# Two heads' maxima products side by side in TensorE's rows, stacks filled by 24 copies, y clipped by max(0, x)

## The chip, the cores and the metric

The kernel runs on one core of one Trainium2 chip. The metric is device time in microseconds of one execution of the whole program. TensorE (PE in the profile, PEld for its weight loads), VectorE (DVE), ScalarE (ACT) and GpSimd (POOL) compute; SyncE (SP) issues nearly all copies.

## The reference

For each of 32 batch entries (128 channels by 512 positions): layer norm over the positions, an attention of 8 heads of 16 channels against a context (rotary positions on half of each head's channels), a residual, a second layer norm, and a feed-forward block whose weights are rounded to -1, 0, 1 and whose activations are rounded to 8 bits.

```
q, k, v = project(layernorm(x)), project(ctx), project(ctx)    # 8 heads x 16 channels, T = 512
scores  = rope(q) . rope(k) / 4 ;  p = softmax(scores) ;  x += Wo (p v)
s       = 128 / max|x'|  per row ;  x'q = clip(round(x' s), -128, 127)     # x' = layernorm(x)
gate,up = x'q . ternary(Wg), x'q . ternary(Wu)       # 2048 columns
y       = fwht(silu(gate) * up)                      # Hadamard transform over 2048
out     = x + clip(round(y s), -128, 127) . ternary(Wd)
```

## The kernel before, in words

Each engine has one program, written out by hand as a list of calls in `step(t)`; a call names its batch entry (`t - 2`, `t + 1` and so on), and all engines walk through their steps in order. Four to five batch entries are in work at the same time. Nothing but semaphores ties the engines together, so the order within each list decides who waits for whom.

- **Products in bf16 pieces.** q and k are split into three bf16 parts each. Six copies of 16 rows (`Q_TERMS`, `K_TERMS`) stack them in `q_stack` and `k_stack`, so that one product over 96 rows gives the six largest cross terms. `stack_part` (L314) makes 12 copies of 128 KB per batch entry: six when part 0 is ready, four for part 1, two for part 2. Part 2 is the last one, made by GpSimd's `third_part` (L1321).
- **Maxima.** `score_max` (L439) multiplies the stacks for one head and 128 queries into a PSUM bank `s1[0]` or `s1[1]`, in turn; `reduce_scores` (L1009) on VectorE takes the row maximum. There are 32 of each per batch entry. `max_transpose` (L451) turns the maxima once all 32 are there, `max_out` (ScalarE) negates them, and `stack_max` (L334) copies them as row 97 of `q_stack`.
- **Softmax.** `scores` (L469) multiplies 97 rows, so that the maximum is already subtracted; ScalarE takes the exponential (L712); `weigh` (L484) multiplies by v. Each `weigh` is four products of 17 columns that run in four column strips of TensorE.
- **After the softmax.** `normalise` (L1019, L1022) on VectorE, `mix` (L1298) on GpSimd, `turn_back` (L1029) on VectorE, `attn_out` (L493) on TensorE, `residual` (L1040 to L1045) on VectorE, then quantisation of x, gate and up products (L525), `half_gates` (L1095), `glu` (L1104) on VectorE and `gate_product` (L1274) on GpSimd.
- **Hadamard transform.** GpSimd makes the outer four stages: `hadamard_half` (L1265, L1266) and `hadamard_last` (L1263); TensorE the inner seven (`hadamard`, L536). `y_out` (L764) brings them to SBUF, `quantise` (L1116 to L1120) finds the scale, `round_y` and `whole_y` (L753) round on ScalarE, `clip_y` (L1128) takes the minimum with 127 on VectorE, `y_transpose` (L547) and `down` (L560) follow.
- **Rotary positions.** `rope_sin` (L989), two copies that exchange 32-row blocks (`shift`, L326), `rope_cos` (L998), and GpSimd's `turn` (L1308), `rest` (L1315) and `third_part` (L1321) make the parts of the next batch entry.

GpSimd's list for one step is: `gate_product` 0 and 1, `hadamard_half` 0, `turn`, `gate_product` 2 and 3, `rest`, `hadamard_half` 1, `mix` 0, `third_part`, `mix` 1, `hadamard_last` 0 and 1, `rstd2`.

## Time and profile before

| what | value |
|---|---|
| median of 3 runs | 1534.24 us (1532.8 to 1534.24) |
| the profiled execution's own time | 1531.52 us |
| its span, first to last instruction | 1529.7 us |
| TensorE busy / VectorE / ScalarE / GpSimd | 1424.7 / 1322.4 / 1082.5 / 1098.7 us |
| mean granted TensorE clock | 0.974 of full |

The busy times are sums over the span; matmuls are pipelined, so two that follow each other overlap in their records, and a busy TensorE is not one at its peak. The span is a start of some 74 us up to the first transpose of maxima, 31 periods between such transposes, and an end of some 97 us.

### The profile page before, as it was taken

To read this page: it belongs to the slowest core of one execution; us is meant where nothing else is said; L and a number is where in the kernel's file an instruction comes from. 1 tells how busy PE (TensorE), PEld (TensorE's weight loads), DVE (VectorE), ACT (ScalarE), POOL (GpSimd) and SP (SyncE) were. 2 spreads that over 40 slices of the span, in tenths; PEclk is the share of its full clock that TensorE was granted. 3 is DMA by queue.
4 is the path that set the end of the run, shared out by engine and by line. 5 is a ranking of instruction groups with operands and counts; after the bars stand their busy time and mean duration, and the time that the engine had idled before them with its cause. 6 is when DMAs were issued, how large, how long until landed. Compare 5 with 4: busy or idle time off the path is not lost.

```text
span 1529.7 us, 30990 instructions
## 1 busy us (share of the span) xinstructions
PE 1424.7 (93%) x11042; PEld 743.8 (49%) x11042; DVE 1322.4 (86%) x2331; ACT 1082.5 (71%) x1777; POOL 1098.7 (72%) x812
## 2 busy tenths in 40 slices
PE   1688999999999999999999999999999999999983
PEld 1215455545555555455555544555555444555442
DVE  2768899999999999999999999999999999998641
ACT  3586677778777777787777777877777777777762
POOL 4124777887777778877777788777777887777674
PEclk9688999999999999999999999999999999999996
DMA  8861434434234344343244443332434443323000
GB/s 211 223 124 37 66 63 77 70 63 69 61 60 77 63 77 76 58 70 63 58 76 63 77 77 61 66 65 61 70 64 77 77 68 59 69 46 47 15 8 14
DMA packets 81112, 108.12 MB, mean 71 GB/s; under 512 B 9664, under 2 KB 59200, under 8 KB 79936
## 3 DMA queue, kind: packets, MB, share of 16 engines
q1 hardware_dynamic: 77744, 93.56, 35.4%
q10 hardware_dynamic: 3216, 12.58, 2.3%
q8 instruction: 89, 1.46, 0.4%
q14 instruction: 63, 0.52, 0.1%
HBM read 38.73 MB, written 8.39 MB: 31 GB/s over the span
## 4 chain that ended last, share of the span: by engine, by line
PE 71%; ACT 12%; DVE 5%; issue 4%; POOL 4%; DMA 2%; SPq 0%; POOLq 0%; ACTq 0%; DVEq 0%
PE s L469 12%; PE ring L525 12%; PE pv L484 12%; PE s L439 11%; PE ring L560 7%; PE ring L536 6%; ACT region L712 4%; PE ring L413 3%; PE ring L493 2%; ACT parts L779 2%; PE ring L547 2%; PE ring L427 2%; ACT y_last L753 1%; ACT y_last L771 1%; DVE maxima L1009 1%
## 5 line engine op out<-in xcount | busy, mean ns | idle before, releaser
L1009 DVE TENSOR_REDUCE maxima<-s 128x1 bf16<-128x512 f32 x1024 | 668.3, 682 | 60.1 <-PE s L439 55.6
L712 ACT ACTIVATE region<-s 128x512 f32<-128x512 f32 x1024 | 576.0, 597 | 133.3 <-PE s L469 123.8
L439 PE MATMUL s<-region 96*128 96x512 bf16 x1024 | 374.3, 391 | 21.7 <-DVE maxima L1009 11.5
L1274 POOL TENSOR_TENSOR region<-region,th 128x512 f32<-128x512 f32 x128 | 161.8, 1273 | 297.1 <-DVE th L1104 295.3
L469 PE MATMUL s<-region 97*128 97x512 bf16 x1024 | 362.2, 384 | 10.0 <-ACT region L712 4.8
L1265 POOL TENSOR_TENSOR region<-region 128x512 f32<-128x512 f32 x192 | 260.3, 1356 | 12.8
L484 PE MATMUL pv<-region,v_ext 128*17 128x512 f32 x2048 | 264.1, 599 | 0.0
L1266 POOL TENSOR_TENSOR region<-region 128x512 f32<-128x512 f32 x192 | 243.9, 1270 | 0.0
L439 PEld LDWEIGHTS s<-region 96*128 96x128 bf16 x1024 | 99.8, 98 | 198.6 <-DVE maxima L1009 74.2
L469 PEld LDWEIGHTS s<-region 97*128 97x128 bf16 x1024 | 93.2, 98 | 187.7 <-ACT region L712 154.1
L1263 POOL TENSOR_TENSOR region<-region 128x1024 f32<-128x1024 f32 x64 | 149.4, 2355 | 0.1
L794 ACT ACTIVATE v_ext<-ring 128x512 f32<-128x512 f32 x32 | 19.1, 598 | 180.7 <-PE ring L427 178.2
L536 PE MATMUL ring<-late_const,region 128*128 128x128 f32 x1024 | 132.7, 279 | 13.7 <-POOL region L1263 11.7
L525 PEld LDWEIGHTS ring<-xqT,wg 128*128 128x128 bf16 x2048 | 123.5, 98 | 42.5 <-issue 16.7
L525 PEld LDWEIGHTS ring<-xqT,wu 128*128 128x128 bf16 x2048 | 122.4, 98 | 44.7 <-issue 26.6
L525 PE MATMUL ring<-xqT,wg 128*128 128x128 bf16 x2048 | 136.0, 219 | 7.4 <-ACT xqT L721 6.9
L536 PEld LDWEIGHTS ring<-late_const,region 128*128 128x128 f32 x1024 | 129.0, 195 | 18.0 <-issue 13.6
L525 PE MATMUL ring<-xqT,wu 128*128 128x128 bf16 x2048 | 135.7, 219 | 2.2 <-ACT y_last L771 1.2
L560 PE MATMUL ring<-wd,y_last 128*128 128x512 bf16 x512 | 127.6, 382 | 1.6 <-ACT y_last L771 1.6
L1095 DVE TENSOR_TENSOR region<-ring,half_gate 128x512 f32<-128x512 f32 x128 | 87.5, 684 | 13.5 <-PE ring L525 9.5
L1308 POOL TENSOR_TENSOR region<-region,rope_c 64x1024 f32<-64x1024 f32 x32 | 75.6, 2362 | 31.5 <-DVE region L998 17.4
L1104 DVE SCALAR_TENSOR_TENSOR th<-th,ring 128x512 f32<-128x512 f32 x128 | 87.3, 682 | 5.5 <-PE ring L525 4.2
(104 smaller groups left out, 1812.0 us busy)
## 6 DMA issues: line engine op xcount, KB each, us to landing
region<-parts SPq DMA_DIRECT2D x384, 128.0 KB, 4.8
x_in<-in_x SPq DMA_DIRECT2D x32, 256.0 KB, 2.6
c_in<-in_ctx SPq DMA_DIRECT2D x32, 256.0 KB, 2.9
rope_c<-region SPq DMA_DIRECT2D x64, 128.0 KB, 2.4
x_res<-in_x SPq DMA_DIRECT2D x32, 256.0 KB, 2.6
out<-o_sb SPq DMA_DIRECT2D x32, 256.0 KB, 2.4
region<-in_wg_t ACTq DMA_DIRECT2D x1, 2048.0 KB, 9.2
region<-in_wu_t ACTq DMA_DIRECT2D x1, 2048.0 KB, 7.3
```

The source lines that it names most:

```text
L439: pe.matmul(s1[p][:, :], q_stack[k][0:STACK, h, 128 * c:128 * (c + 1)], k_stack[k][0:STACK, h, :], start=True, stop=True).then_inc(s1_full ...
L469: pe.matmul(s2[n % 2][:, :], k_stack[k][0:STACK + 1, h, 128 * c:128 * (c + 1)], q_stack[k][0:STACK + 1, h, :], start=True, stop=True).then ...
L484: last = pe.matmul(pv[32 * i:32 * i + DH + 1, :], v_ext[b % 2][:, c, 4 * g + i, :], probs[:, (4 * u + i) % 8, :], start=(c == 0), stop=(c ...
L525: last = pe.matmul(bank(f"{name}{j}")[:, 128 * i:128 * (i + 1)], w[:, c, o:o + 128], xqT[:, c, :], start=(c == 0), stop=(c == HC - 1), ski ...
L536: last = pe.matmul(bank(f"y{j}")[:, 128 * c:128 * (c + 1)], z[:, o:o + 128], had[:, :], start=True, stop=True, skip_group_check=True)
L560: last = pe.matmul(bank("down")[:, :], yqT[:, c, :], wd[:, c, :], start=(c == 0), stop=(c == IC - 1))
L712: act.activation(probs[:, n % 8, :], s2[n % 2][:, :], ACT.Exp, scale=SCALE).then_inc(exp_done, 1)
L1009: dve.reduce_max(maxima[:, c, h:h + 1], s1[p][:, :], AXX).then_inc(s1_max[p], 1)
L1263: return pool.tensor_tensor(o[:, :, half, :], a[:, :, 0, :], a[:, :, 1, :], ALU.subtract if half else ALU.add)
L1265: pool.tensor_tensor(o[:, :, 0, :], a[:, :, 0, :], a[:, :, 1, :], ALU.add)
L1266: return pool.tensor_tensor(o[:, :, 1, :], a[:, :, 0, :], a[:, :, 1, :], ALU.subtract)
L1274: pool.tensor_tensor(zj, zj, th[:, j % 2, :], ALU.mult).then_inc(glu_done, 1)
```

## The change

Seven things change together.

- The maxima use only the four largest cross terms, which fill 64 rows. Heads 0 to 3 have theirs in rows 0 to 63 of the stacks, heads 4 to 7 in rows 64 to 127, and `score_max` issues two products, one in each half of TensorE's rows, into the two PSUM banks. It waits for both banks first.
- The other two terms of heads 0 to 3 lie in rows 64 to 95, and those of heads 4 to 7 in rows 32 to 63. The maximum is row 96 for the former and row 31 for the latter; rows 0 to 31 of the latter's `q_stack` are set to zero once. `scores` multiplies 97 or 128 rows.
- Each copy of `stack_part` becomes two of half the size (24 in all), `shift` issues four copies and covers all 128 rows, `stack_max` issues two. `rope_sin` and `turn` work on 128 rows.
- `whole_y` and `clip_y` become one ScalarE instruction, `below_top`, which writes max(0, top - y) with top = ROUND + 127; `yT_out` turns that back with scale -1 and bias 127.
- For the last batch entry, VectorE does the second half of the gate products and of the Hadamard stages (`tail_half`).
- GpSimd fills the first two stacks completely at the start, not one row of them.
- The lists of all engines are in a new order, and the PSUM ring is assigned anew.

```diff
-STACK_DMAS = 2 * len(Q_TERMS)
-SHIFTS = 2
+STACK_DMAS = 4 * len(Q_TERMS)
+SHIFTS = 4
+MAX_ROW = (STACK, 31)
+ROWS = (slice(0, STACK + 1), slice(0, 128))
+MAIN = (slice(0, 4 * DH), slice(4 * DH, 8 * DH))
+HALF = NH // 2
+def term_rows(g, r):
+    lo = DH * r if g == 0 else 64 + DH * r if r < 4 else 32 + DH * (r - 4)
+    return slice(lo, lo + DH)
+def heads(g):
+    return slice(HALF * g, HALF * (g + 1))
...
                         if terms[r] == part:
-                            sp.dma_start(dst[DH * r:DH * (r + 1), :, :], parts[:, part, w, :]).then_inc(stacked, 16)
+                            for g in range(2):
+                                sp.dma_start(dst[term_rows(g, r), heads(g), :],
+                                             parts[64 * g:64 * (g + 1), part, w, :]).then_inc(stacked, 16)
...
-                wait(pe, s1_max[p], 16 * b + i)
-                pe.matmul(s1[p][:, :], q_stack[k][0:STACK, h, 128 * c:128 * (c + 1)],
-                          k_stack[k][0:STACK, h, :], start=True, stop=True).then_inc(s1_full[p], 1)
+                for g in range(2):
+                    wait(pe, s1_max[g], 16 * b + i)
+                for g in range(2):
+                    h = HALF * g + i // KC
+                    pe.matmul(s1[g][:, :], q_stack[k][MAIN[g], h, 128 * c:128 * (c + 1)],
+                              k_stack[k][MAIN[g], h, :], start=True, stop=True).then_inc(s1_full[g], 1)
...
-                pe.matmul(s2[n % 2][:, :], k_stack[k][0:STACK + 1, h, 128 * c:128 * (c + 1)],
-                          q_stack[k][0:STACK + 1, h, :], start=True, stop=True).then_inc(s2_full, 1)
+                rows = ROWS[h // HALF]
+                pe.matmul(s2[n % 2][:, :], k_stack[k][rows, h, 128 * c:128 * (c + 1)], q_stack[k][rows, h, :],
+                          start=True, stop=True).then_inc(s2_full, 1)
...
-            def whole_y(b, j):
+            def below_top(b, j):
...
-                act.activation(yq[:, 1024 * j:1024 * (j + 1)], ys[:, 1024 * j:1024 * (j + 1)], ACT.Copy, bias=-ROUND) \
-                   .then_inc(whole, 1)
+                act.activation(yq[:, 1024 * j:1024 * (j + 1)], ys[:, 1024 * j:1024 * (j + 1)], ACT.Relu, scale=-1.0,
+                               bias=top[:, :]).then_inc(yq_done, 1)
...
+            def tail_half(b):
+                if b != B - 1:
+                    return
+                for j in (2, 3):
+                    moved(dve, f"gate{j}", b)
+                    moved(dve, f"up{j}", b)
+                    zj = z[:, 512 * j:512 * (j + 1)]
+                    dve.tensor_tensor(zj, zj, th[:, j % 2, :], ALU.mult).then_inc(tail_steps, 1)
+                dve.wait_ge(tail_steps, 2)
+                dve.wait_ge(had16_done, 2 * b)
+                for stage in range(3):
+                    butterfly(dve, stage, 1).then_inc(tail_steps, 1)
+                    dve.wait_ge(tail_steps, 3 + stage)
+                dve.wait_ge(had8_steps, 6 * b + 3)
+                butterfly(dve, 3, 1).then_inc(tail_done, 1)
...
-                pool.memset(k_stack[k][STACK:STACK + 1, :, :], 1.0).then_inc(ones_rows_set, 1)
...
+                    pool.memset(k_stack[k][:, :, :], 1.0).then_inc(ones_rows_set, 1)
+                    pool.memset(q_stack[k][0:32, heads(1), :], 0.0).then_inc(ones_rows_set, 1)
```

The first place is VectorE's list from the transpose of the mixed attention (`turn_back`) to the statistics of the residual. Before, it reads as follows; `maxima<-s_0` and `maxima<-s_1` are `reduce_scores` from the two banks, `o_sb` is the store of the entry before.

```order
1041 L1009 TENSOR_REDUCE maxima<-s_1 128x1
1042 L1009 TENSOR_REDUCE maxima<-s_0 128x1
1043 L1029 STREAM_TRANSPOSE attn<-mixed 128x512
1044 L1136 SCALAR_TENSOR_TENSOR o_sb<-ring,sc,h_res 128x512
1045 L1009 TENSOR_REDUCE maxima<-s_1 128x1
1046 L1040 SCALAR_TENSOR_TENSOR h_res<-ring,out_bias,x_res 128x512
1047 L1042 BN_STATS st<-h_res 128x6
1048 L1043 BN_AGGR mv<-st 128x2
1049 L1045 TENSOR_SCALAR ve<-mv 128x1
1050 L1009 TENSOR_REDUCE maxima<-s_0 128x1
1051 L1051 TENSOR_REDUCE sc<-turned_pv 128x1
```

In the changed kernel the same stretch of VectorE's list reads:

```order
1019 L1037 TENSOR_REDUCE maxima<-s_0 128x1
1020 L1037 TENSOR_REDUCE maxima<-s_1 128x1
1021 L1057 STREAM_TRANSPOSE attn<-mixed 128x512
1022 L1174 SCALAR_TENSOR_TENSOR o_sb<-ring,sc,h_res 128x512
1023 L1037 TENSOR_REDUCE maxima<-s_0 128x1
1024 L1037 TENSOR_REDUCE maxima<-s_1 128x1
1025 L1068 SCALAR_TENSOR_TENSOR h_res<-ring,out_bias,x_res 128x512
1026 L1070 BN_STATS st<-h_res 128x6
1027 L1071 BN_AGGR mv<-st 128x2
1028 L1073 TENSOR_SCALAR ve<-mv 128x1
1029 L1037 TENSOR_REDUCE maxima<-s_0 128x1
1030 L1079 TENSOR_REDUCE sc<-turned_pv 128x1
```

Between `turn_back` and `residual` there stood one reduction, and now there stand two. From there up to the first `glu` both lists hold the same instructions in a slightly other order, with four reductions in each.

The second place is TensorE's list around the transpose of the maxima (`eye_b,maxima`). Before:

```order
1048 L439 MATMUL s_1<-region 128x512
1049 L493 MATMUL ring<-attn,late_const 128x512
1050 L427 MATMUL ring<-table_const,c_in 128x128 x4
1051 L536 MATMUL ring<-late_const,region 128x128 x4
1052 L451 MATMUL ring<-eye_b,maxima 8x128 x4
1053 L439 MATMUL s_0<-region 128x512
1054 L536 MATMUL ring<-late_const,region 128x128 x4
1055 L439 MATMUL s_1<-region 128x512
1056 L439 MATMUL s_0<-region 128x512
1057 L536 MATMUL ring<-late_const,region 128x128 x8
```

In the changed kernel, with the waits of each instruction in brackets (a matmul that waits stands in a row apart from those behind it in its group):

```order
1120 L480 MATMUL s_0<-region 128x512 [waits s1_max1,s1_max0]
1121 L480 MATMUL s_1<-region 128x512
1122 L531 MATMUL ring<-attn,late_const 128x512 [waits attn_done,ring_free1]
1123 L577 MATMUL ring<-late_const,region 128x128 [waits had16_done,ring_free2]
1124 L577 MATMUL ring<-late_const,region 128x128 x3
1125 L492 MATMUL ring<-eye_b,maxima 8x128 [waits s1_max1,s1_max0,ring_free0]
1126 L492 MATMUL ring<-eye_b,maxima 8x128 x3
1127 L480 MATMUL s_0<-region 128x512 [waits s1_max1,s1_max0,stacked]
1128 L480 MATMUL s_1<-region 128x512
1129 L577 MATMUL ring<-late_const,region 128x128 [waits had16_done,ring_free1]
```

The maxima products now come in pairs behind one wait for both banks. The first pair of a batch entry stands ahead of the second Hadamard group, as its single product did, and waits for all copies of that entry's stacks.

The third place is SP's list for one batch entry, before:

```order
104 L334 DMA region<-neg_max 1x8x512
105 L297 DMA x_res<-in_x 128x512
106 L326 DMA rope_c<-region 32x1024 x2
107 L341 DMA out<-o_sb 128x512
108 L314 DMA region<-parts 16x8x512 x12
```

and in the changed kernel:

```order
100 L362 DMA rope_c<-region 32x1024 x4
101 L349 DMA region<-parts 16x4x512 x24
102 L371 DMA region<-neg_max 1x4x512 x2
103 L331 DMA x_res<-in_x 128x512
104 L379 DMA out<-o_sb 128x512
```

SP issues 30 copies for shifts, stacks and maxima of one entry, where it issued 15.

## Rows read from the trace of the kernel before

**Rows 1.** The page: busy us (share of the span) and instructions of two engines

```profile
PE 1424.7 (93%) x11042; PEld 743.8 (49%) x11042; DVE 1322.4 (86%) x2331; ACT 1082.5 (71%) x1777; POOL 1098.7 (72%) x812
```

**Rows 2.** One period: busy us (instructions) per engine, clock, DMA; then all maxima transposes

```profile
951.50:995.10 43.60, 43.07 (x345) 22.59 (x343) 40.60 (x73) 32.35 (x54) 33.99 (x27) 1.00 0.38 68
L451 PE MATMUL ring<-eye_b,maxima x128: 219/219/314, 73.9 to 1432.9; 128*8 128x128 bf16 x128
```

**Rows 3.** Timeline of TensorE around one `weigh` and two products of maxima and scores

```profile
702.92 0.38 PE L469 MATMUL s<-region 97*128 97x512 bf16 x1
703.23 1.05 PE L484 MATMUL pv<-region,v_ext 128*17 128x512 f32 x8
704.21 1.07 PE L525 MATMUL ring<-xqT,wu 128*128 128x128 bf16 x16
...
705.12 0.38 PE L439 MATMUL s<-region 96*128 96x512 bf16 x1
705.34 0.38 PE L469 MATMUL s<-region 97*128 97x512 bf16 x1
```

**Rows 4.** Timeline of VectorE from `turn_back` to the first `glu`

```profile
951.64 0.71 DVE L1029 STREAM_TRANSPOSE attn<-mixed 128x512 f32<-128x512 f32 x1
...
956.12 0.69 DVE L1009 TENSOR_REDUCE maxima<-s 128x1 bf16<-128x512 f32 x1 [0.43 <-PE s L439]
...
964.17 0.68 DVE L1009 TENSOR_REDUCE maxima<-s 128x1 bf16<-128x512 f32 x1
964.77 0.68 DVE L1095 TENSOR_TENSOR region<-ring,half_gate 128x512 f32<-128x512 f32 x1
965.37 0.68 DVE L1104 SCALAR_TENSOR_TENSOR th<-th,ring 128x512 f32<-128x512 f32 x1
```

**Rows 5.** Timeline of GpSimd from the first gate product to behind the second `mix`

```profile
966.19 2.60 POOL L1274 TENSOR_TENSOR region<-region,th 128x512 f32<-128x512 f32 x2 [9.01 <-DVE th L1104]
...
974.02 1.80 POOL L1265 TENSOR_TENSOR region<-region 128x512 f32<-128x512 f32 x1
975.79 1.26 POOL L1266 TENSOR_TENSOR region<-region 128x512 f32<-128x512 f32 x1
...
995.07 4.67 POOL L1263 TENSOR_TENSOR region<-region 128x1024 f32<-128x1024 f32 x2
```

**Rows 6.** Groups over 19 periods: busy us, mean ns, idle before

```profile
L1308 POOL TENSOR_TENSOR region<-region,rope_c 64x1024 f32<-64x1024 f32 x19 | 44.9, 2363 | 1.5
...
L1128 DVE TENSOR_SCALAR y_last<-y_last 128x1024 bf16<-128x1024 bf16 x38 | 44.6, 1175 | 0.0
```

**Rows 7.** SP's copies of part 2 in one period, and TensorE's first maxima product

```profile
L314 SPq DMA_DIRECT2D region<-parts x2: 546/573/600, 951.0 to 951.6; - x2
...
DMA to landing us min/median/max: 3.3/3.4/3.5
955.62 0.39 PE L439 MATMUL s<-region 96*128 96x512 bf16 x1
```

**Rows 8.** Start: fills and first rstd on GpSimd, the first stack's copies, their landing

```profile
1.27 7.07 POOL L1233 MEMSET region<- 1x4096 bf16 x2
...
24.24 7.77 SPq L314 DMA_DIRECT2D region<-parts  x12
DMA to landing us min/median/max: 3.4/5.9/8.5
L1240 POOL MEMSET region<- x1: 3516/3516/3516, 94.5 to 94.5; 128x4096 bf16 x1
```

**Rows 9.** End: the last Hadamard half on VectorE's and GpSimd's timeline, then TensorE

```profile
1488.40 0.69 DVE L1104 SCALAR_TENSOR_TENSOR th<-th,ring 128x512 f32<-128x512 f32 x1 [1.31 <-PE ring L525]
...
1492.28 2.49 POOL L1274 TENSOR_TENSOR region<-region,th 128x512 f32<-128x512 f32 x2
...
1502.53 4.64 POOL L1263 TENSOR_TENSOR region<-region 128x1024 f32<-128x1024 f32 x2
1505.01 6.42 PE L536 MATMUL ring<-late_const,region 128*128 128x128 f32 x32 [11.32 <-POOL region L1263]
```

496 lines of the change are left out of this document (241 added, 255 removed).

## The prediction

> **What bounds the kernel now.** I read the page's busy table first, then one steady period by windows, then the timelines of three engines over that period, and last the start and the end.
>
> The page puts TensorE first (93%) and VectorE close behind [rows 1]. In a steady period of 43.6 us they are busy 43.07 and 40.60 us [rows 2], so both are nearly full, while ScalarE and GpSimd have 10 us to spare. The first transpose of maxima stands 73.9 us into the span, the last at 1432.9 [rows 2]: 31 periods with a mean of 43.8, a little over the steady 43.6.
>
> A full engine is not yet the bound. GpSimd idles once per period, 9.01 us, for the first `glu` [rows 5], and from there it works without a break until the second `mix` ends. That closes a loop. `turn_back` on VectorE starts at 951.64, the first `glu` at 965.37 [rows 4], the first gate product at 966.19, and `hadamard_last`, which follows the second `mix`, at 995.07 [rows 5]. The next `turn_back` needs that `mix`. From 951.64 to 966.19 is 14.55 us, from 966.19 to 995.07 is 28.88, and some 0.15 us of handing over make 43.58: the whole period. The only idle time shown inside it is 0.43 us on VectorE, where the first reduction waits for TensorE [rows 4]. So the kernel has two bounds of the same size, TensorE's list and this loop, and the reader should see that relieving one alone brings nothing.
>
> **TensorE, the pairs.** Two products of 512 columns stand 0.22 us apart [rows 3], so a pair of them costs 0.44 us, and 16 pairs 7.0 us per period. Side by side they cost 0.22 and save 3.5 us per period, if changing to half rows is free. The nearest row to what such a change costs is `weigh`, the step into four column strips: it starts 0.31 us behind the product ahead, not 0.22 (0.09 more), and what follows starts 0.98 us later, though eight f32 products in two rounds of four are worth 0.86 by the spacing of two 0.43 us rounds (0.12 more) [rows 3]. The 0.43 is my estimate for an f32 product of 512 columns, twice the bf16 spacing. By that row a pair costs 0.22 + 0.09 + 0.12 = 0.43 us, what it costs today. Six of the 16 pairs stand next to a `weigh` or the transpose, where one change serves both, 0.1 us each. So the pairs save between 0.6 us (change charged) and 3.5 us (free) per period. I take 0.6, since the row for columns is the nearest.
>
> The Trainium skill, TensorEngine Tiling (Array Packing), Key Properties, says that going from one tiling mode to another drains the array; the 0.09 and 0.12 us agree for column strips, and no row here shows it for row halves. By that rule the saving is the 0.6; by the same page's ideal of twice the speed it would be the 3.5.
>
> **VectorE.** Two clips go. They cost 44.6 us over 19 periods, 2.35 per period [rows 6], and VectorE falls to about 38.3. One of them also lies inside the loop: one `hadamard_half` instruction takes 1.80 us where its neighbour takes 1.26 [rows 5], because a clip of 0.4 us starts in it. That is -0.53 in the loop. `turn` takes 2.36 us on 64 rows [rows 6], and `hadamard_last` with as many columns on 128 rows 4.67 for two [rows 5], so `turn`, and by the same reason `rope_sin`, costs nothing more on 128 rows; `below_top` has the size of `whole_y`.
>
> **The loop.** One more reduction stands between `turn_back` and `residual`: +0.60 us, the spacing of two such instructions [rows 4]. The idle 0.43 us depends on the first maxima product, at 955.62 [rows 7]. It now waits for four copies of part 2, not two. They are issued about 0.6 us apart, the second at 951.6, and land up to 3.5 us later [rows 7]; the fourth lands at 951.6 + 1.2 + 3.5 = 956.3, 0.7 us later than the product started. Since VectorE also comes 0.6 us later, the idle time stays near 0.5. If the half-size copies land sooner the idle time vanishes. So the loop is 43.58 + 0.60 - 0.53, then +0.1 or -0.4: 43.2 to 43.8. I take 43.5, near the upper half, since 24 issues and two more for the maxima keep SP busier. TensorE's list needs about 43.0 by the charged price, and is covered by the loop. The steady part gives 31 x (43.5 - 43.56) = -2 us (bounds -11 to +7).
>
> Pairs also end the alternation of banks: VectorE idles from the end of one pair to the arrival of the next, about 0.5 us, where no other work stands between. The list has four such places, 2 us, and none is inside the loop; VectorE has 5 us to spare, so I cost it at nothing. If that cover went, it would be those 2 us a period.
>
> **The start.** GpSimd fills two single rows in 7.07 us before the first rstd [rows 8]. A fill of all 128 rows takes the same 3.5 us each [rows 8], but two fills of 2048 columns come on top, by halves 1.8 us each: +3.6. The first stack's 12 copies are issued over 7.77 us and the last lands 8.5 us after its issue [rows 8], so 39.9; 24 copies take 15.5 us to issue and the last then lands about 3.4 us later, 43.1, plus what started late, 47; but the weights' traffic, which slowed the old ones, is over by then. Between +2 and +7; I take +4.
>
> **The end.** VectorE takes the second half of the last entry. The last `glu` starts at 1488.40, GpSimd begins the second half at 1492.28 and ends the third stage at 1502.53, TensorE starts at 1505.01 [rows 9]. VectorE needs 8 instructions of 0.60 and one of about 1.2, so 6.0 us, from 1489.1 to about 1495.5; GpSimd's first half has ended by 1492.28 [rows 9]. Then one last stage each, 2.3 us on GpSimd: TensorE starts near 1497, 8 us sooner. The bound against it: the 1.80 us instruction shows that the two engines can block each other [rows 5]; if they take turns throughout, TensorE starts near 1501, 4 us sooner. A gain of 3 us more is possible if TensorE's clock holds: its 32 products take 6.42 us here. I take -8 (bounds -4 to -11).
>
> The Trainium skill, SBUF — State Buffer, SBUF: two separate sides, says that VectorE with two SBUF inputs and GpSimd exclude each other for whole instructions. By it the end would give the 4 us. The trace shows such a stop for the clip alone.
>
> **The sum.** 1531.5 + 4 - 2 - 8 = 1525.5 for the profiled execution. The median of the runs lies 2.7 us above that execution, so 1528. What this kernel's measurement can tell from no change is about 0.2%, 3 us.
>
> **The rivals.**
>
> - *The relief of TensorE counts in full.* The pairs are free and the loop is softer than I read it. TensorE's list falls to 43.56 - 3.5 = 40.1, VectorE to 38.3. If the period gets half way, 41.8, the time is 1528 - 31 x 1.7 = 1475. For it: TensorE is 99% busy; against it: the loop adds up to the period without rest.
> - *The change of mode costs more for rows than for columns.* The second half's weights of 128 columns are loaded behind the change. TensorE's list decides once it passes the loop's 43.5, that is when a pair costs over 0.46. At 0.50 the list is 44.1: 1528 + 31 x 0.6 = 1547. For it: `weigh` loads only 17 columns per strip and still pays; against it: six neighbours share a change.
> - *Copies come late.* If a copy of half size lands no faster than a whole one, 24 of them at 1.1 us, the spacing I estimate from the growing delays of the first stack (3.4 to 8.5 us over 12 copies issued 0.65 apart), take 26 us of the period, the first product waits some 4 us, and 31 x 3 makes 1620.
> - *The pairs don't overlap at all.* Then each costs 0.65, the list 46.9, and the time 1528 + 31 x 3.4 = 1633.
>
> **Chances.** Loop-bound as forecast 0.48, with a range of its own of 1517 to 1540; full relief 0.20; dearer change of mode 0.22; late copies 0.06; no overlap 0.04. The range that leaves out 2 in 10 goes from 1480 to 1555. Faster: 0.31 of the forecast's share, all of the relief and a little, 0.53; same 0.14; slower 0.33.
>
> **What would show it.** Right: the period stays between 43.2 and 43.8 while VectorE's busy time per period drops by 2 us; GpSimd still waits about 9 us for the first `glu` and for nothing else; the pair's two products start within 0.02 us of each other, 0.31 us behind the one ahead; the instruction of 1.80 us is 1.27; TensorE's last Hadamard group starts 8 us nearer to its gate products. Wrong: a period under 43, or GpSimd idle at another place; TensorE without gaps and a period over 44; waits for the copies at the first pair.

## The result, and the profile of the changed kernel

The changed kernel took 1540.81 us (median of 5 runs, 1538.71 to 1543.81), the kernel before 1532.8 us (5 runs, 1531.79 to 1534.24). The ratio is 1.0051, 95% interval 1.0034 to 1.0068: slower, by half a per cent. The profiled execution took 1540.81 us, over a span of 1539.0 us.

The page's table of busy times, which answers to [rows 1], and the lines that make up the chain that ended last:

```profile
PE 1383.7 (90%) x11042; PEld 698.3 (45%) x11042; DVE 1264.9 (82%) x2277; ACT 1100.2 (71%) x1777; POOL 1077.0 (70%) x806
...
SPq L349 16%; PE ring L563 13%; PE s L507 9%; PE pv L522 7%; PE s L480 6%; PE ring L451 4%; DVE maxima L1037 3%; DMA region<-parts 3%; POOL region L312 2%; POOL region L311 2%; PE ring L577 2%; DMA rope_c<-region 2%; PE ring L601 1%; ACT re
```

TensorE has 41 us less to do and VectorE 57.5 us less, and the kernel is slower. L349, SyncE's 24 copies, makes up 16% of the chain. One period by windows, and all transposes of maxima (L492 is what L451 was), as in [rows 2]:

```profile
702.00:745.50 43.50, 42.12 (x346) 21.31 (x345) 38.58 (x71) 32.99 (x54) 33.38 (x26) 1.00 0.24 73
L492 PE MATMUL ring<-eye_b,maxima x128: 218/219/314, 85.7 to 1447.1; 128*8 128x128 bf16 x128
```

TensorE and VectorE are each a microsecond or two freer within a period of the same length. With the starts of the transposes the span falls into four pieces:

| piece | before | changed | difference | predicted |
|---|---|---|---|---|
| up to the first transpose | 73.9 | 85.7 | +11.8 | |
| first three periods together | 140.1 | 138.3 | -1.8 | start as a whole +4 |
| the other 28 periods | 1218.7 | 1222.9 | +4.2 | -2 |
| from the last transpose on | 97.0 | 92.1 | -4.9 | -8 |

The sum is +9.3 us, the difference of the spans (1529.7 and 1539.0). Of the +4.2 us, 1.6 lie in 24 periods of 43.66 us (43.59 before) and 2.6 in the last four, two of which take 44.22 and 44.97 us; no run looks into those. The prediction's error of 15.3 us (1525.5 for the profiled execution, 1540.8 measured) is 6 at the start, 6 in the periods and 3 at the end.

**The period.** VectorE from `turn_back` (L1057) to the first `glu` (L1132), which answers to [rows 4]:

```profile
701.49 0.70 DVE L1057 STREAM_TRANSPOSE attn<-mixed 128x512 f32<-128x512 f32 x1
...
702.77 1.29 DVE L1037 TENSOR_REDUCE maxima<-s 128x1 bf16<-128x512 f32 x2
...
705.84 0.69 DVE L1037 TENSOR_REDUCE maxima<-s 128x1 bf16<-128x512 f32 x1
...
709.05 0.54 DVE L1008 TENSOR_SCALAR xn<-x_in,mv,rs 128x512 f32<-128x512 f32 x1
709.51 0.42 DVE L1109 TENSOR_SCALAR xq<-turned_pv 128x512 bf16<-128x512 f32 x1
...
715.24 0.68 DVE L1132 SCALAR_TENSOR_TENSOR th<-th,ring 128x512 f32<-128x512 f32 x1
```

and GpSimd, as in [rows 5]; the first line is the second `mix` of the kernel before, which followed GpSimd's work without a wait, and the others are the changed kernel's:

```profile
994.49 0.61 POOL L1298 TENSOR_TENSOR mixed<-turned_pv,inv_sum 128x256 f32<-128x256 f32 x1
...
700.52 0.62 POOL L1327 TENSOR_TENSOR mixed<-turned_pv,inv_sum 128x256 f32<-128x256 f32 x1 [0.40 <-DVE inv_sum L1050]
...
716.07 2.51 POOL L1299 TENSOR_TENSOR region<-region,th 128x512 f32<-128x512 f32 x2 [9.01 <-DVE th L1132]
...
723.81 1.27 POOL L311 TENSOR_TENSOR region<-region 128x512 f32<-128x512 f32 x1
```

From `turn_back` to the gate product it is 14.58 us, as it was (14.55); the means between 300 and 1250 us are 14.68 and 14.56. The third of GpSimd's stages, which took 1.80 us beside a clip, takes 1.27 (723.81). The wait of 0.43 us ahead of the first reduction is gone (705.84 follows without a gap), a reduction came in, and `xn`, the normalised x of the next entry, stands ahead of `xq`, where it stood behind `quantise` before. On GpSimd the second `mix` now waits 0.40 us (0.24 us a period by the waits view from 400 to 1200) for `inv_sum`, which VectorE makes once TensorE's last `weigh` of the entry is done.

That wait shows a second loop, which the prediction did not follow: from `turn_back` over `xq` and TensorE's list to the last `weigh`, and over `inv_sum` and the second `mix` back to the next `turn_back`. Its legs, from start to start, are means over the entries whose `turn_back` lies between 350 and 1200 us:

| leg, mean us | before | changed | g3_xq_first | h1_combined |
|---|---|---|---|---|
| `turn_back` to `xq` (VectorE) | 7.51 | 8.10 | 7.75 | 7.63 |
| `xq` to its transposes (TensorE) | 0.56 | 0.57 | 0.57 | 0.57 |
| transposes to the last `weigh` | 32.32 | 32.25 | 32.30 | 32.30 |
| last `weigh` to `inv_sum` | 1.41 | 1.41 | 1.41 | 1.41 |
| `inv_sum` to the second `mix` | 1.04 | 0.38 | 0.41 | 0.46 |
| second `mix` to the next `turn_back` | 0.73 | 0.95 | 0.92 | 0.91 |

Before, `inv_sum` was ready some 0.7 us before GpSimd came to it (1.04 less the 0.38 that the handing over takes where GpSimd waits). The reduction and `xn` ahead of `xq` have taken that up, and GpSimd now waits.

TensorE around the first pairs of an entry (L480 the pairs, L492 the transpose of maxima, L539 that of xq), beside [rows 3, 7]:

```profile
704.66 0.39 PE L492 MATMUL ring<-eye_b,maxima 128*8 128x128 bf16 x4
705.20 0.39 PE L480 MATMUL s<-region 64*128 64x512 bf16 x2 [0.16 <-DMA region<-parts]
705.52 2.94 PE L577 MATMUL ring<-late_const,region 128*128 128x128 f32 x24
708.84 0.60 PE L507 MATMUL s<-region 97*128 97x512 bf16 x2 [0.37 <-DMA region<-neg_max]
710.07 0.38 PE L539 MATMUL ring<-eye_b,xq 128*128 128x128 bf16 x4 [0.63 <-DVE xq L1109]
...
710.67 0.39 PE L480 MATMUL s<-region 64*128 64x512 bf16 x2
710.99 0.61 PE L507 MATMUL s<-region 97*128 97x512 bf16 x2
```

A pair is two products in one row of 0.39 us, which start 2 to 6 ns apart, and the next instruction starts 0.32 us after it. What TensorE now waits for in 800 us (400 to 1200), by the waits view: line, what it waited for, us in total, times, longest:

```profile
PE ring L539 <- DVE xq L1109: 16.3, 19, 1.3
PE s L480 <- DMA region<-parts: 5.7, 11, 1.1
...
PE s L507 <- DMA region<-neg_max: 2.6, 8, 0.8
```

The kernel before has two rows there, 3.5 us for `xqT` and 0.2 us for the maxima. The relief of TensorE, about 1 us a period, is spent in waits: 0.9 us for `xq`, 0.3 us for copies of the stacks.

**The start**, beside [rows 8]; L362 are the shifts, L1337 the rotation, L349 the copies:

```profile
7.15 0.42 ACTq L290 DMA_DIRECT2D region<-in_wg_t  x1
...
17.67 2.92 SPq L362 DMA_DIRECT2D rope_c<-region  x4
...
25.20 2.34 POOL L1337 TENSOR_TENSOR region<-region,rope_c 128x1024 f32<-128x1024 f32 x1 [12.88 <-DMA rope_c<-region]
28.76 15.27 SPq L349 DMA_DIRECT2D region<-parts  x24
...
51.20 0.39 ACTq L290 DMA_DIRECT2D region<-in_wd_t  x1
...
56.17 2.46 SPq L362 DMA_DIRECT2D rope_c<-region  x4
...
67.33 2.34 POOL L1337 TENSOR_TENSOR region<-region,rope_c 128x1024 f32<-128x1024 f32 x1 [24.44 <-DMA rope_c<-region]
...
76.12 1.87 PE L418 MATMUL pv<-absum,ones 128*128 128x1 f32 x8 [3.28 <-ACT wu L716]
```

The first stack is 5.9 us later (its first product at 45.88, before at 39.97): the rotation starts 4.5 us later (25.20, before 20.75), and the 24 copies add the rest. From there to the first transpose another 5.9 us are lost. The second entry's rotation starts at 67.33; in the kernel before it started at 54.57, ahead of the down weights:

```profile
50.27 1.21 SPq L326 DMA_DIRECT2D rope_c<-region  x2
54.57 2.33 POOL L1308 TENSOR_TENSOR region<-region,rope_c 64x1024 f32<-64x1024 f32 x1 [17.43 <-DVE region L998]
60.47 0.39 ACTq L269 DMA_DIRECT2D region<-in_wd_t  x1
```

**The end**, beside [rows 9]; L1142 are VectorE's gate products, L309 the last stage:

```profile
1497.05 2.50 POOL L1299 TENSOR_TENSOR region<-region,th 128x512 f32<-128x512 f32 x2 [8.81 <-DVE th L1132]
...
1504.56 2.36 DVE L1142 TENSOR_TENSOR region<-region,th 128x512 f32<-128x512 f32 x2
1504.78 1.59 POOL L311 TENSOR_TENSOR region<-region 128x512 f32<-128x512 f32 x1
1506.33 1.71 POOL L312 TENSOR_TENSOR region<-region 128x512 f32<-128x512 f32 x1
1506.95 1.64 DVE L311 TENSOR_TENSOR region<-region 128x512 f32<-128x512 f32 x1
...
1512.02 3.29 POOL L309 TENSOR_TENSOR region<-region 128x1024 f32<-128x1024 f32 x1 [3.98 <-DVE region L312]
1515.46 5.81 PE L577 MATMUL ring<-late_const,region 128*128 128x128 f32 x32 [5.26 <-POOL region L309]
```

### The profile page after: what moved, and what is told of

Its sections match the earlier page's. It is cut to its first block, busy times and chain, and to the rows that moved or that the text cites. A ratio compares the mean times of both kernels' runs of the same rounds, so it can differ in the third digit from the quotient of the medians.

```text
span 1539.0 us, 31895 instructions
## 1 busy us (share of the span) xinstructions
PE 1383.7 (90%) x11042; PEld 698.3 (45%) x11042; DVE 1264.9 (82%) x2277; ACT 1100.2 (71%) x1777; POOL 1077.0 (70%) x806
## 4 chain that ended last, share of the span: by engine, by line
PE 45%; SPq 17%; DVE 10%; POOL 9%; issue 7%; ACT 6%; DMA 5%; POOLq 0%; DVEq 0%; ACTq 0%
SPq L349 16%; PE ring L563 13%; PE s L507 9%; PE pv L522 7%; PE s L480 6%; PE ring L451 4%; DVE maxima L1037 3%; DMA region<-parts 3%; POOL region L312 2%; POOL region L311 2%; PE ring L577 2%; DMA rope_c<-region 2%; PE ring L601 1%; ACT region L737 1%; ACT parts L806 1%
## 5 line engine op out<-in xcount | busy, mean ns | idle before, releaser
L1037 DVE TENSOR_REDUCE maxima<-s 128x1 bf16<-128x512 f32 x1024 | 660.8, 683 | 122.4 <-PE s L480 114.8
L507 PE MATMUL s<-region 128*128 128x512 bf16 (+1 forms) x1024 | 356.2, 387 | 22.1 <-DMA region<-neg_max 12.9
L311 POOL TENSOR_TENSOR region<-region 128x512 f32<-128x512 f32 x189 | 240.4, 1272 | 12.5
L480 PE MATMUL s<-region 64*128 64x512 bf16 x1024 | 204.1, 394 | 42.0 <-DVE maxima L1037 24.0
L312 POOL TENSOR_TENSOR region<-region 128x512 f32<-128x512 f32 x189 | 241.2, 1276 | 0.0
L507 PEld LDWEIGHTS s<-region 128*128 128x128 bf16 (+1 forms) x1024 | 89.8, 97 | 251.5 <-ACT region L737 147.7
L480 PEld LDWEIGHTS s<-region 64*128 64x128 bf16 x1024 | 50.8, 93 | 226.6 <-issue 140.4
L309 POOL TENSOR_TENSOR region<-region 128x1024 f32<-128x1024 f32 x63 | 147.9, 2368 | 4.0 <-DVE region L312 4.0
L791 ACT ACTIVATE region<-ring 128x512 f32<-128x512 f32 x128 | 75.7, 592 | 95.6 <-PE ring L577 95.2
L577 PEld LDWEIGHTS ring<-late_const,region 128*128 128x128 f32 x1024 | 121.1, 194 | 35.2 <-issue 27.8
L1337 POOL TENSOR_TENSOR region<-region,rope_c 128x1024 f32<-128x1024 f32 x32 | 75.4, 2357 | 48.9 <-DMA rope_c<-region 47.0
L761 ACT ACTIVATE th<-region 128x512 f32<-128x512 f32 x128 | 80.4, 628 | 27.0 <-DVE region L1123 26.9
```

The lines of the kernel that those rows point to most:

```text
L309: return engine.tensor_tensor(o[:, :, half, :], a[:, :, 0, :], a[:, :, 1, :], ALU.subtract if half else ALU.add)
L311: engine.tensor_tensor(o[:, :, 0, :], a[:, :, 0, :], a[:, :, 1, :], ALU.add)
L312: return engine.tensor_tensor(o[:, :, 1, :], a[:, :, 0, :], a[:, :, 1, :], ALU.subtract)
L480: pe.matmul(s1[g][:, :], q_stack[k][MAIN[g], h, 128 * c:128 * (c + 1)], k_stack[k][MAIN[g], h, :], start=True, stop=True).then_inc(s1_full ...
L507: pe.matmul(s2[n % 2][:, :], k_stack[k][rows, h, 128 * c:128 * (c + 1)], q_stack[k][rows, h, :], start=True, stop=True).then_inc(s2_full, 1)
L577: last = pe.matmul(bank(f"y{j}")[:, 128 * c:128 * (c + 1)], z[:, o:o + 128], had[:, :], start=True, stop=True, skip_group_check=True)
```

## The experiments

Each is an edit of the changed kernel (one, and its extension, of the kernel before). The time of the kernel before, run beside them, had medians of 1533.1 to 1534.2 us. "First" is the start of the first transpose of maxima in the profiled execution, "period" the mean of the 24 periods from the fourth on, both from the starts of those transposes. One profiled execution gives the period to about 0.05 us: edits that touch the start alone left it between 43.64 and 43.74. The start scatters more: f1, g3 and h2, whose edits don't touch what the first transpose needs, have it at 84.5, 84.8 and 86.7, so a difference of 1 us in that column says nothing.

| kernel | median us | ratio to before, 95% | first | period |
|---|---|---|---|---|
| before | 1532.8 | 1 | 73.9 | 43.59 |
| changed | 1540.8 | 1.0034 to 1.0068 | 85.7 | 43.66 |
| e1_split_first | 1541.4 | 1.0035 to 1.0063 | 85.2 | 43.74 |
| e2_split_all | 1539.6 | 1.0028 to 1.0055 | 84.6 | 43.68 |
| e3_late_fills | 1537.5 | 1.0013 to 1.0034 | 84.7 | 43.64 |
| e4_full_rows | 1550.9 | 1.0104 to 1.0132 | 86.0 | 44.02 |
| f1_fewer_products | 1534.3 | 0.9994 to 1.0011 | 84.5 | 43.58 |
| f2_reductions_later | 1594.9 | 1.0364 to 1.0402 | 86.6 | 45.38 |
| f3_four_more_issues | 1666.5 | 1.0838 to 1.0873 | 89.0 | 47.84 |
| f4_four_from_scalar | 1662.2 | 1.0817 to 1.0846 | 86.1 | 47.75 |
| g1_late_load_split | 1536.1 | 1.0011 to 1.0029 | 79.8 | 43.72 |
| g2_two_from_scalar | 1536.3 | 1.0012 to 1.0031 | 82.2 | 43.59 |
| g3_xq_first | 1531.0 | 0.9972 to 0.9990 | 84.8 | 43.37 |
| g4_clip_alone | 1529.8 | 0.9974 to 0.9993 | 74.6 | 43.49 |
| h1_combined | 1522.5 | 0.9906 to 0.9934 | 80.8 | 43.26 |
| h2_no_tail | 1544.1 | 1.0056 to 1.0084 | 86.7 | 43.68 |
| h3_before_clip_tail | 1524.1 | 0.9927 to 0.9952 | 73.9 | 43.49 |
| h4_combined_fewer | 1517.3 | 0.9874 to 0.9904 | 79.9 | 43.12 |

**e1_split_first.** The first suspicion for the start was the wait for both banks: with no other work on VectorE a pair came only every 2.06 us (VectorE's reductions at 46.52 and 48.58).

```diff
-                for g in range(2):
-                    wait(pe, s1_max[g], 16 * b + i)
+                if b > 0:
+                    for g in range(2):
+                        wait(pe, s1_max[g], 16 * b + i)
                 for g in range(2):
+                    if b == 0:
+                        wait(pe, s1_max[g], 16 * b + i)
```

> The changed kernel; for the first entry alone each product for the maxima waits only for its own bank, right before it, not for both banks ahead of both. Theory (the start lost the alternation of banks: pairs 2.06 us apart where 1.36 would do): the first transpose of maxima comes 4 to 6 us sooner than 85.7 and the time falls by as much, 1535 to 1537, periods unchanged. Rival (at the start the low clock and the row mode of the products set the pace, not the wait for both banks): under 1 us, 1540 to 1541.

The reductions then came every 1.39 us per pair, and nothing was gained: after the last of them VectorE waited 8.3 us for the next pair, which stands in TensorE's list behind the sum over the up weights.

```profile
59.65 9.04 DVE L1040 TENSOR_REDUCE maxima<-s 128x1 bf16<-128x512 f32 x13
...
75.61 1.87 PE L418 MATMUL pv<-absum,ones 128*128 128x1 f32 x8 [7.65 <-ACT wu L719]
...
78.06 1.29 DVE L1040 TENSOR_REDUCE maxima<-s 128x1 bf16<-128x512 f32 x2 [8.29 <-PE s L483]
```

The theory falls: the wait for both banks is real, but another wait covers it.

**e2_split_all.** The same for all entries.

```diff
-                for g in range(2):
-                    wait(pe, s1_max[g], 16 * b + i)
                 for g in range(2):
+                    wait(pe, s1_max[g], 16 * b + i)
```

> The changed kernel with the wait of each bank right before its own product, for all entries, so that two products need not start together. Theory (the steady periods are set by the chain of copies, loop and GpSimd, and VectorE's wait for pairs has slack): the start gains as in the first experiment and the period stays within 0.05 us of 43.66: 1534 to 1537. Rival (the lost alternation costs 0.1 us a period and more): period 43.5 or less, 1530 or less. Second rival (two products that no longer overlap cost TensorE 0.1 to 0.2 us for each of 16 neighbours and TensorE's list is the bound): period 44.5 or more, 1560 or more.

1539.6 us and a period of 43.68: neither the alternation nor the common start matters at this size. The 1 us of the median is within what the runs scatter.

**e3_late_fills.** GpSimd fills behind its first power of the variance.

```diff
-                ones_rows(t + 6, 0)
-                ones_rows(t + 6, 1)
                 rstd1(t + 1)
+                ones_rows(t + 1, 0)
+                ones_rows(t, 1)
```

> The changed kernel; GpSimd fills the rows of ones of the first two stacks behind its first power of the variance, not ahead of it. Theory (the fills delay the first entry by 3.3 us): first transpose of maxima 2.5 to 3.5 us sooner, 1537 to 1538.5. Rival (the first stack is set by the 24 issues and what is ahead of them, and the fills now come between GpSimd's power and its sum): no gain, 1540 to 1542.

The power came at 5.37, not 11.77, and the rotation at 25.00, not 25.20:

```profile
5.37 0.56 POOL L1282 TENSOR_TENSOR rs<-ve,half_neg 128x1 f32<-128x1 f32 x1 [4.23 <-DVE ve L1001]
...
5.97 5.44 DVE L1008 TENSOR_SCALAR xn<-x_in,mv,rs 128x512 f32<-128x512 f32 x1 [0.77 <-POOL rs L1282]
...
16.18 2.58 SPq L362 DMA_DIRECT2D rope_c<-region  x4
25.00 2.34 POOL L1337 TENSOR_TENSOR region<-region,rope_c 128x1024 f32<-128x1024 f32 x1 [13.88 <-DMA rope_c<-region]
```

GpSimd fills from 5.88 to 11.12. VectorE's L1008, 0.55 us elsewhere, took 5.44 us: it ended about when the two fills did. And the shifts were issued 1.5 us sooner and still landed at 25.0, while 4 MB of gate weights (issued from 7.58 on) came in. So 1.5 of the 3.3 us by which the shifts are issued later than before (17.67, before 14.34) cost the first stack next to nothing: sooner issues met the same traffic. No run leaves the fills out altogether, and what the other 1.8 us cost isn't shown. The median is 3.3 us lower; the first transpose is 1.1 us sooner, which is within its scatter, and where the rest comes from isn't shown.

**e4_full_rows.** The maxima from all six terms, over 96 or 128 rows.

```diff
+FULL = (slice(0, STACK), slice(0, 128))
-                    pe.matmul(s1[g][:, :], q_stack[k][MAIN[g], h, 128 * c:128 * (c + 1)],
-                              k_stack[k][MAIN[g], h, :], start=True, stop=True)
+                    pe.matmul(s1[g][:, :], q_stack[k][FULL[g], h, 128 * c:128 * (c + 1)],
+                              k_stack[k][FULL[g], h, :], start=True, stop=True)
```

> The changed kernel, but each product for the maxima reads 96 rows (heads 0 to 7) or all 128 (heads 8 to 15), six terms rather than the four largest, so that two products cannot lie side by side and no row mode is entered or left; the rows ahead of heads 8 to 15 add an old maximum, so the maxima of these heads differ from the reference's. Theory (the loop and not TensorE's list bounds the period): 16 pairs cost 0.44 rather than 0.41, TensorE's busy time rises by 0.3 to 0.6 us a period and the period by 0.3 at most: 1541 to 1552. Rival (TensorE's list bounds it): the period rises by the whole, and if lying side by side is worth what two 0.22 us products in the time of one are worth (3.5 us a period), to 47: 1640.

Period +0.36 us, 10 us in all. By windows from 400 to 1200 TensorE is busy 775.46 us (42.67 a period) here and 770.85 us (42.07) in the changed kernel. Lying side by side is thus worth 0.6 us of TensorE's time a period, as the prediction took it, and not 3.5. TensorE's leg of the second loop is 32.66 us, 0.41 longer, and the second `mix` waits 9.1 us in 800, not 4.4.

**f1_fewer_products.** 0.9 us less for TensorE; a quarter of the down projection's sum is left out.

```diff
-                down(t - 4, 4, 8)
```

> The changed kernel without four of the 16 products of the down projection, so that its sums lack a quarter: 0.9 us less on TensorE's list in a period, nothing else. If TensorE's list is the bound: period 42.8, 1513. If a loop that runs through other engines is (VectorE and GpSimd, or the 24 copies): the four products stood in a stretch that waits anyway, period within 0.2 of 43.6, 1535 to 1541.

Period 43.58, 0.08 below. Of the 6.5 us by the medians, 2.3 lie behind the last transpose (89.8 us, not 92.1); another 1.2 lie ahead of the first, where none of these products stands, and are scatter. About half of what went came back as a new wait, 8.6 us in 800 for exponentials, and TensorE's leg of the second loop is only 0.13 us shorter (32.12). So the sum of TensorE's work doesn't set the period of the changed kernel; what counts is the time from `xq` to the last `weigh`.

**f2_reductions_later.** Two reductions out of the loop.

```diff
                 half_gates(t - 2, 0)
-                reduce_scores(t, 2)
                 round_piece(t - 2, 2, 6)
-                reduce_scores(t, 3)
                 half_gates(t - 2, 1)
                 glu(t - 2, 0)
                 round_piece(t, 0, 3)
+                reduce_scores(t, 2)
+                reduce_scores(t, 3)
```

> The changed kernel; VectorE's reductions 2 and 3 come behind its first product of tanh and up, not ahead of it, which takes 1.2 us out of the loop from the turned back attention to GpSimd's first gate product. If that loop bounds the period: 43.1 to 43.3, 1526 to 1531. If the 24 copies or TensorE's list bound it: no change of the period, 1539 to 1542, or 0.1 to 0.5 us worse where TensorE's next pair waits for the reductions that come later, up to 1557.

54 us slower, more than either side expected. The waits of TensorE from 400 to 1200:

```profile
PE s L480 <- DVE maxima L1037: 32.8, 36, 1.7
```

TensorE's waits for reductions are 1.9 us a period, where they were 0.2, and the period grew by 1.7. That doesn't test the loop; it shows that with one wait for two banks, a reduction can't be put off past the next pair.

**f3_four_more_issues.** The same bytes in 28 copies.

```diff
-STACK_DMAS = 4 * len(Q_TERMS)
+STACK_DMAS = 4 * len(Q_TERMS) + 4
...
+                                if part == 0 and r < 2 and w == 0:
+                                    lo = term_rows(g, r).start
+                                    for j in range(2):
+                                        sp.dma_start(dst[lo + 8 * j:lo + 8 * (j + 1), heads(g), :],
+                                                     parts[64 * g + 32 * j:64 * g + 32 * (j + 1), part, w, :]) \
+                                          .then_inc(stacked, 16)
+                                    continue
```

> The changed kernel; four of part 0's copies are cut into halves, so that SyncE issues 28 copies of the same bytes rather than 24: at 0.63 us an issue the last lands 2.5 us later. If the chain of copies bounds the period (the first pair waits 0.16 us for the last copy): period +2.4, 1615. If the loop through VectorE and GpSimd does and the first pair can be late without harm: under +0.3 a period, up to 1550. In between if the pair's lateness eats other slack first.

Each period is 4.2 us longer: more than the 2.5 us of the issues. TensorE's waits from 400 to 1200, then its timeline:

```profile
PE s L487 <- DMA region<-parts: 56.2, 17, 4.1
...
763.91 0.39 PE L487 MATMUL s<-region 64*128 64x512 bf16 x2 [2.77 <-DMA region<-parts]
764.23 4.57 PE L584 MATMUL ring<-late_const,region 128*128 128x128 f32 x24
```

The first pair waits 3.4 us a period for copies, and behind such a wait the 24 Hadamard products take 4.57 us, where the changed kernel took 2.94. The granted clock, 1.00 in that stretch of the changed kernel, is 0.63 from 763.90 to 768.50 here and 1.00 on either side: behind this idle time of 2.8 us TensorE runs for a while at the lower of its two levels, 1.2 rather than 2.4 GHz. The 2.5 us of the issues and the 1.6 us of the slower products nearly make up the 4.2. So the copies had no slack (0.16 us of waiting in the period shown), and here a late copy costs its lateness and two thirds again.

**f4_four_from_scalar.** Four copies issued by ScalarE.

```diff
+                                if part == 0 and r < 2 and w == 0:
+                                    continue
...
+            def act_copies(b):
...
+                for r in range(2):
+                    for g in range(2):
+                        act.dma_start(q_stack[slot(b)][term_rows(g, r), heads(g), :],
+                                      parts[64 * g:64 * (g + 1), 0, 0, :]).then_inc(stacked, 16)
...
                 first_part(t + 1)
+                act_copies(t + 1)
```

> The changed kernel; four of part 0's copies are issued by ScalarE right behind its first part, not by SyncE, so that the last copy lands 2.5 us sooner and ScalarE's queue is 1.6 to 2.5 us fuller at its weak spot. If the chain of copies bounds the period: 43.2 to 43.4, 1527 to 1534. If it doesn't: period unchanged, 1535 to 1541 (the first stack may still be 2 us sooner at the start), or worse where the exponentials behind the issues are awaited.

The waits for copies are gone (0.2 us in 800), and 44.7 us for exponentials came in their place. ScalarE's timeline has the reason:

```profile
742.39 2.50 ACTq L822 DMA_DIRECT2D region<-parts  x4
744.94 2.98 ACT L739 ACTIVATE region<-s 128x512 f32<-128x512 f32 x5 [2.68 <-issue]
```

Four issues hold ScalarE's whole list for 2.7 us at a place where TensorE's next scores wait for exponentials. The second `mix` then waits 58.1 us in 800 for `inv_sum`, and the period is 4.1 us longer: the rival, at its dearest.

**g1_late_load_split.** With e1's edit, the first 2 MB of the down weights are loaded later.

```diff
-                load_weights(t, 2, 0)
                 round_y(t - 3, 1)
...
                 first_part(t + 1)
+                load_weights(t, 2, 0)
```

> The changed kernel with the split waits of the first entry, and the first half of the down weights (2 MB) loaded behind the second entry's first part in ScalarE's order, not ahead of it. Theory (the first transpose of maxima is late since the second entry's shifts, 56.2 to 58.6, share the DMA engines with that load of 51.2 and land at 67.3; ScalarE then stands at the first part, and the sum over the up weights behind it): shifts land before 63, first transpose of maxima at 79 to 82 in place of 85.7, 1534 to 1538. Rival (the up weights alone fill the DMA engines, the shifts land no sooner): 85, 1539 to 1541.

```profile
54.16 2.74 SPq L362 DMA_DIRECT2D rope_c<-region  x4
...
61.39 2.34 POOL L1340 TENSOR_TENSOR region<-region,rope_c 128x1024 f32<-128x1024 f32 x1 [20.03 <-DMA rope_c<-region]
```

From the first issue to the rotation it is now 7.2 us, not 11.2; the issue itself is 2.0 us sooner. With e1's edit alone the issue was 0.8 us sooner (55.37) and the rotation stood at 66.8. The first transpose stands at 79.8, 5.9 us sooner, as much as had been lost between the first stack and it. The time fell by 4.7.

**g2_two_from_scalar.** Two copies of part 2 in ScalarE's idle time ahead of `v_out`, with the same waits as in f4 and one for part 2.

```diff
+                            if part == 2 and w == 1:
+                                continue
...
+                act_copies(t)
                 v_out(t)
```

> The changed kernel; two of the four copies of part 2 are issued by ScalarE in its idle time of 3.4 us ahead of the values' copy, the other two by SyncE, so that the last lands 1.2 us sooner and nothing waits behind ScalarE's two. Theory A (two chains are equal within 0.2 us in a period: copies, and VectorE with GpSimd; 28 issues made each period 4.1 us longer, so the copies have no slack): the waits of pairs for copies (0.3 us a period) go, period 43.3 to 43.6, 1528 to 1539. Theory B (the copies alone bound the period): 42.6 or less, 1510. Rival (issuing from ScalarE costs what its exponentials lose, as with four of part 0): over 1545.

4.5 us faster than the changed kernel, 3.5 of them before the first transpose (82.2) and at most 0.07 us a period. 0.07 us is hardly above the scatter of the period. Theory A stands as far as this goes; the same kind of edit as f4, at another place of the same list, costs nothing that shows.

**g3_xq_first.** One line moved.

```diff
                 gate_factors(t - 2)
-                norm1_apply(t + 1)
                 quant_x(t - 2)
+                norm1_apply(t + 1)
```

> The changed kernel; VectorE rounds the attention's sum to xq ahead of the next entry's normalised x, not behind it: the loop from the turned back attention through xq, its transposes and gate 0 to GpSimd's first gate product is 0.46 us shorter, nothing else moves. If that loop bounds the period alone: 43.2, 1527. If the copies are as tight (theory of two equal chains): 43.4 to 43.66, 1532 to 1541.

9.8 us faster than the changed kernel, period 43.37, so 0.29 of the 0.46 us came through. It did not come where the expectation had it: from `turn_back` to the first gate product the mean is 14.75 us (14.68 in the changed kernel), for VectorE still does the same work there. What became shorter is `turn_back` to `xq`, 7.75 rather than 8.10 us; TensorE's wait for `xq` over 800 us fell from 16.3 to 10.5 us, and the second `mix` no longer waits for `inv_sum`. This is the clearest test of the second loop: an edit that moves 0.46 us within VectorE's list, at 38.6 busy of 43.5, is worth more than 0.9 us off TensorE.

**g4_clip_alone.** In the kernel before.

```diff
-                act.activation(yq[:, 1024 * j:1024 * (j + 1)], ys[:, 1024 * j:1024 * (j + 1)], ACT.Copy, bias=-ROUND) \
-                   .then_inc(whole, 1)
+                act.activation(yq[:, 1024 * j:1024 * (j + 1)], ys[:, 1024 * j:1024 * (j + 1)], ACT.Relu, scale=-1.0,
+                               bias=top[:, :]).then_inc(yq_done, 1)
...
-                clip_y(t - 3, 1)
...
-                clip_y(t - 2, 0)
```

> The kernel before with one part of the change: y is clipped by ScalarE's max(0, x) and VectorE's two minima of a period go (2.35 us of VectorE), all else in its old order. Theory (VectorE has slack and the minima stand outside the loop but for what they excluded GpSimd, 0.5 us): period 43.1 to 43.56, 1517 to 1534. Rival (no slack anywhere, VectorE's whole time counts): 41.2 bounded by TensorE's 43.07, 1517 or less.

3.3 us faster than the kernel before that ran beside it (1529.8 and 1533.1), period 43.49. VectorE loses 2 us of work a period, and 0.1 comes through. GpSimd is done sooner: from the first gate product to the end of the second `mix` it takes 0.5 us less, but `turn_back` then starts 0.57 us behind that end, not 0.11. It follows reductions in VectorE's list, and these wait for TensorE (60.9 us in 800, before 21.6), which is busy 42.9 of 43.49 us. That TensorE's list holds the rest back is read from these waits; no run tests it.

**h1_combined.** The edits of e1, e3, g1, g2 and g3 together.

> The changed kernel with the five edits that each gave something or were free: xq ahead of the normalised x, two copies from ScalarE, the late load of down weights, split waits for the first entry, the late fills. If they add: start 79 to 80 or less in place of 85.7, period 43.2 to 43.3, 1522 to 1526. If one resource is left right behind them (TensorE's list of about 43.1, or the copies), the period stays at 43.3 and more and only the start adds: 1525 to 1530.

1522.5 us: 18 us below the changed kernel and 0.8% below the kernel before. TensorE's waits from 400 to 1200:

```profile
PE ring L544 <- DVE xq L1129: 9.7, 18, 0.8
PE s L512 <- DMA region<-neg_max: 4.4, 18, 0.3
```

No pair waits for copies any more. The start adds less than hoped (80.8), the periods add in full (43.26). The second `mix` waits for nothing here: `turn_back` to the first gate product takes 14.65 us, from there to the next `turn_back` 28.62, and the sum of 43.27 is the predicted loop again.

**h2_no_tail.** The last entry's second half back on GpSimd.

```diff
-                tail_half(t - 2)
...
-                if b == B - 1 and j > 1:
-                    pe.wait_ge(tail_done, 1)
-                else:
-                    pe.wait_ge(had16_done, 2 * b + 1 + j // 2)
+                pe.wait_ge(had16_done, 2 * b + 1 + j // 2)
```

> The changed kernel with GpSimd alone for the last entry's second half, as before the change. Theory (the shared tail saved 4.8 us between the gate products and the last Hadamard products): end 4 to 5 us longer, 1544 to 1546. Rival (the shorter end comes from elsewhere): 1540 to 1542.

The stretch behind the last transpose is 97.1 us, as before the change (97.0) and not 92.1. The shorter end is the tail's, all of it. By the medians the kernel is 3.3 us slower than the changed one, somewhat less than the 5.0 us of this stretch.

**h3_before_clip_tail.** g4's kernel with `tail_half` as in the changed one.

> The kernel before with the clip by ScalarE's max(0, x) and the last entry's second half on VectorE, but 96 rows for each head, one head at a time, 12 copies and the old orders. Theory (these two parts gain 3.3 and 4 to 5 us, and the pairs with their copies and orders lose what is left of the change): 1524 to 1527. Rival (the two gains overlap or the tail's needs the new order): 1528 to 1531.

1524.1 us. Two small parts of the change, without the pairs, the 24 copies and the new orders, make the kernel 0.6% faster; what the rest adds to them is 17 us.

**h4_combined_fewer.** The combined kernel with f1's edit.

> The combined kernel without four of the 16 products of the down projection (its sums lack a quarter): 0.9 us less on TensorE's list in a period. If after the shorter loop TensorE's list of 43.1 is what stands next: period 42.5 to 42.8, some 15 us below the combined one. If copies or the loop do: period within 0.2 of the combined one, 0 to 6 us below it.

5.2 us below the combined one, period 43.12, 0.14 less for 0.9 us off TensorE. About half of the 0.9 us is again a wait for exponentials (8.5 us in 800).

## Why the prediction was wrong

The range held the time, the sign did not. By its steps:

- *The start, +4*: the step that failed most, by 6 us. The sum had a term for the fills (+3.6) and one for the copies of the first stack, and together they reach the +5.9 us that the first stack lost, though the parts are others: it is late through four shifts that are issued over 2.9 us among the weights' traffic (rotation +4.5 us), and through 24 issues. Moving the fills brought 0.2 us (e3). The other 5.9 us had no term at all: the new order of ScalarE issues 2 MB of down weights at 51.2, ahead of the second entry's shifts at 56.2 (before: shifts at 50.3, weights at 60.5), and the chain from the rotation through ScalarE's list to the sum over the up weights ends at the first transpose (g1: 5.9 us back). I had said that the weights' traffic was over by then; that was so for the copies of the first stack only, which landed 2.4 to 2.6 us after their issue.
- *"I take 43.5", a steady part of -2 us*: measured 43.66 and +4.2. The step that failed is "TensorE's list needs about 43.0 by the charged price, and is covered by the loop". The loop's own terms were right: the reduction came in, the clip went, and the idle 0.43 us vanished, which makes 43.58 + 0.60 - 0.53 - 0.43 = 43.2. But of the 0.5 us that the clip freed on GpSimd nothing was left, for the second `mix` now waits 0.27 us (mean) for `inv_sum`, and `turn_back` starts 0.2 us later behind it. The path to `inv_sum` runs over `xq` and TensorE's list, and it became 0.59 us longer on VectorE: the added reduction, and `xn`, which the "slightly other order" put ahead of `xq`. g3 moves that one line back, and the period falls by 0.29; e4 makes TensorE's part 0.41 longer, and it rises by 0.36; with all five edits it is 43.26, near the 43.2 of the terms. By its time the steady part is off by 0.16 us a period; 2.6 of the 6 us lie in the last four periods, and their cause is open.
- *Two bounds of equal size, so relieving one brings nothing*: right as to the result. TensorE's list fell from 43.1 to 42.1 us a period and the period stayed. The two are not separate in the changed kernel, though: the loop that closes there runs through VectorE, TensorE and GpSimd.
- *A pair costs 0.43 us*: right. It is entered 0.10 us later than a product of full rows would be and left 0.10 us later (0.32 us to the next, not 0.22), so 0.41 us; its two products start 2 to 6 ns apart. e4 confirms the saving of 0.6 us.
- *VectorE falls to about 38.3*: measured 38.6. *The instruction of 1.80 us becomes 1.27*: right.
- *The copies*: the rival of late copies took 1.1 us a copy; the half-size ones land 2.6 us after their issue, one per issue, so it fell, and my 24 issues of 0.64 us were right. But I gave them no price of their own, since their last landing was to meet the first pair within the loop's other half microsecond. The first pair waits for it, 0.16 us in the period shown and 0.3 us on average, which I had named as a sign of being wrong, and four issues more cost 4.2 us a period (f3). The copies are a third chain of nearly the same length, and the prediction counted two.
- *The end, -8*: the mechanism was right and the size off; -4.9 is near the bound I gave for engines that take turns. They do: GpSimd's stages took 1.59 and 1.71 us beside VectorE's, VectorE's two gate products 1.18 each rather than 0.60 and its first stage 1.64, and GpSimd's last stage, which started beside VectorE's of 1.23, 3.29 against 2.3 alone. VectorE also started late (1504.56 against gate products at 1497.05), behind its last half gate, which waited 3.6 us for TensorE. The Trainium skill, SBUF — State Buffer, SBUF: two separate sides, says that VectorE with two SBUF inputs and a GpSimd instruction that reads SBUF exclude each other for the whole instruction, and the trace agrees with these figures.
- *Alternation of banks at nothing*: right for this order (e2), and e1 shows the same of the start. f2 shows what it costs where a reduction comes too late for the next pair.
- Of the rivals, full relief (0.20) and no overlap are excluded by e4 and by the pairs that start together; the dearer change of mode by the pair's 0.41.

What stays open: how chains that are equal within some 0.3 us share out the last tenths, and what holds `turn_back` 0.2 us back behind the second `mix`. That the shifts land late because of the weights' traffic is shown for the second entry (g1, together with e1's edit); for the first it is argued from e3, since no run moved those loads. The kernels with the clip alone have a first period of 51 us rather than 48; that wasn't pursued.

## What to carry to other kernels

In a kernel with two chains of equal length, a change that relieves one engine is decided by the lines that its new order moves on the other chain, and by what it adds to a queue that had no share in the bound yet: read every reordered line between the ends of the loop, not only those that the change names. And where an engine inside the loop waits for nothing, note how long its inputs had been ready: that margin (0.7 us for `inv_sum` here) is what the next change can use up unseen. Price a copy by its issue (0.64 us on the queue here, for 64 KB as for 128 KB) and by the slack of the one that lands last. In the start, look up which transfers of weights are in flight when each small, awaited transfer is issued.
